# A macaron block on one core: folded sums, values loaded by fours, and finer first and last steps

## What is computed

```python
x = x + 0.5 * ffn(layernorm(x))
x = x + attention(layernorm(x))
x = x + 0.5 * ffn(layernorm(x))

def ffn(x):                    # up (2048, 512), down (512, 2048): only their signs are used
    hidden = relu((x @ sign(up).T) * up_scale)
    return (hidden @ sign(down).T) * down_scale * output_scale

def attention(x):              # 16 heads of 32
    q, k, v = heads(x @ w_q.T), heads(x @ w_k.T), heads(x @ w_v.T)
    return merge(softmax(q @ k.T / sqrt(32)) @ v) @ w_o.T

def layernorm(x):
    return (x - mean(x)) / sqrt(var(x) + 1e-5)
```

## Time and profile before

| | |
|---|---|
| median of 3 runs | 2874.53 us |
| the profiled execution | 2881.08 us |
| its span, first to last instruction | 2879.0 us |
| TensorE busy | 2846.1 us (99%) |
| weight loads | 1949.0 us (68%) |
| vector engine | 2041.4 us (71%) |
| scalar engine | 1607.7 us (56%) |
| POOL | 1372.8 us (48%) |
| DMA packets | 184375, 424.28 MB |

### The profile page before, as it was taken

The page is one execution under the profiler, slowest core; times in us unless marked ns, Lnnn a source line. Parts: engine busy times, 40 slices in busy tenths (PEclk is TensorE's granted clock), DMA queues, the critical chain, the costliest instruction groups (busy, mean ns, idle before and its releaser), DMA issues.

```text
span 2879.0 us, 37964 instructions
## 1 busy us (share of the span) xinstructions
PE 2846.1 (99%) x14288; PEld 1949.0 (68%) x14288; DVE 2041.4 (71%) x3037; ACT 1607.7 (56%) x2850; POOL 1372.8 (48%) x487
## 2 busy tenths in 40 slices
PE   8999999999999999999999999999999999999999
PEld 6888888887755555555555555555555468888887
DVE  5655556768888888888888888888888446555553
ACT  6344434332276767767677777676777654333333
POOL 0000000000089999989898899898988620000000
PEclk9999999999999999999999999999999999999999
DMA  5111112555389999999999999999999962222210
GB/s 190 31 58 30 30 30 71 200 194 188 136 175 194 200 203 202 201 200 203 201 202 204 197 203 202 201 200 200 203 200 204 209 179 59 59 59 59 59 30 30
DMA packets 184375, 424.28 MB, mean 147 GB/s; under 512 B 89728, under 2 KB 90752, under 8 KB 148224
## 3 DMA queue, kind: packets, MB, share of 16 engines
q0 software_dynamic: 31824, 231.75, 39.2%
q1 hardware_dynamic: 152368, 190.11, 24.1%
HBM read 121.91 MB, written 67.63 MB: 66 GB/s over the span
## 4 chain that ended last, share of the span: by engine, by line
PE 84%; DMA 7%; POOL 3%; DVE 3%; issue 2%; ACT 1%; SPq 0%; POOLq 0%; DVEq 0%; ACTq 0%
PE bank L624 16%; PE bank L601 15%; PE bank L1064 15%; PE bank L1060 13%; PE bank L1091 13%; PE bank L743 7%; DMA att_dma_acc<-att_p 3%; PE bank L451 3%; POOL att_acc L924 3%; DMA att_dma_acc<-att_dma_acc 2%; PE bank L1118 1%; DMA prob_sums<-head_total 1%; DMA head_tot_t<-prob_sums 0%; PE bank L240 0%; DMA op_inv_second<-prob_inverse 0%
## 5 line engine op out<-in xcount | busy, mean ns | idle before, releaser
L975 DVE TENSOR_REDUCE att_row_max<-bank 128x1 f32<-128x512 f32 x2048 | 1249.3, 681 | 209.3 <-PE bank L1064 209.1
L924 POOL TENSOR_TENSOR att_acc<-att_acc,att_p 128x2048 f32<-128x2048 f32 x217 | 1079.8, 4976 | 19.7 <-ACT att_p L1044 13.0
L1044 ACT ACTIVATE att_p<-bank 128x512 f32<-128x512 f32 x1792 | 919.4, 617 | 289.3 <-PE bank L1060 286.2
L1064 PE MATMUL bank<-att_k,att_q 96*128 96x512 f32 x2048 | 834.0, 409 | 2.9 <-DVE att_row_max L975 2.6
L1060 PE MATMUL bank<-att_q,att_k 98*128 98x512 f32 x2048 | 810.3, 399 | 6.0 <-ACT att_p L1044 6.0
L1064 PEld LDWEIGHTS bank<-att_k,att_q 96*128 96x128 f32 x2048 | 387.2, 189 | 275.0 <-DVE att_row_max L975 123.2
L1060 PEld LDWEIGHTS bank<-att_q,att_k 98*128 98x128 f32 x2048 | 386.8, 189 | 116.7 <-ACT att_p L1044 17.6
L573 ACT ACTIVATE ffn_hid<-bank,up_s 128x512 f32<-128x512 f32 x256 | 176.3, 689 | 517.2 <-PE bank L601 505.7
L521 DVE TENSOR_TENSOR ffn_hid_lo<-ffn_hid,ffn_hid_hi 128x512 fp32r<-128x512 f32 x256 | 175.7, 691 | 383.7 <-ACT ffn_hid_hi L576 383.7
L1091 PE MATMUL bank<-att_p,att_v 128*32 128x512 f32 x3584 | 434.6, 601 | 0.0
L601 PE MATMUL bank<-hi,ffn_up_w 128*128 128x512 f32 x1024 | 400.7, 391 | 5.7 <-DVE lo L189 3.8
(11 more groups left out here) (116 smaller groups left out, 2378.8 us busy)
## 6 DMA issues: line engine op xcount, KB each, us to landing
att_dma_acc<-att_p POOLq DMA_DIRECT2D x161, 1024.0 KB, 10.6
att_dma_acc<-att_dma_acc POOLq DMA_DIRECT2D x30, 1024.0 KB, 11.9
att_dma_acc<-att_acc POOLq DMA_DIRECT2D x30, 1024.0 KB, 6.9
att_q<-q_hi SPq DMA_DIRECT2D x64, 256.0 KB, 4.1
att_k<-k_hi SPq DMA_DIRECT2D x64, 256.0 KB, 6.7
x<-x_after_ffn SPq DMA_DIRECT2D x15, 1024.0 KB, 7.3
x_after_ffn<-x_out SPq DMA_DIRECT2D x8, 1024.0 KB, 9.9
q_hi<-qkv_o_hi SPq DMA_DIRECT2D x32, 256.0 KB, 2.0
```

What stands on the lines that cost most here:

```text
L924: self.nc.gpsimd.tensor_tensor(self.acc[H % 2][:], a[:], self.tile(H, kt)[:], ALU.add).then_inc(self.summed, 1)
L975: self.nc.vector.tensor_reduce(self.row_max[odd][:, qt, q:q + 1], m[:], axis=AX.X, op=ALU.max).then_inc(self.m_read, 1)
L1044: self.nc.scalar.activation(into[:, q * CH:(q + 1) * CH], self.score_bank(H, kt, q)[:], ACT.Exp, scale=SCALE).then_inc(self.exp_done, 1)
L1064: self.nc.tensor.matmul(m[:], self.q_st[T % NB][0:KQ, qt * P:(qt + 1) * P], self.k_st[T % NB][0:KQ, q * CH:(q + 1) * CH], start=True, stop ...
```

## The change

- Sums over partitions: for 1 < N < 8 and N > 17 (`folded`) the vector engine adds rows 64 to 127 of the sum to rows 0 to 63 (`fold`: add, copy of half the rows to the other half, add of half the rows), writes the high part to rows 0 to 63 and the low part to rows 64 to 127 of one tile (`parts`), and TensorE multiplies that once.
- First chunk: TensorE runs 13 and 9 products of the identity with itself before and after the first mean; the mean is one float32 product of the unsplit sum; the first signs are made in two halves, each ahead of a half of the high part; the norm's later steps stand one hidden tile later.
- First chunk of Q, K, V and of the second FFN: norm steps moved by one tile, later in the one, sooner in the other.
- Attention: values are loaded for four heads at once (`load_values`, eight loads of 1 MB, the first in the last chunk of Q, K, V), into other places; the six loads of Q and K for heads 0 and 1 are spread over tiles; the last head's tile 8 is summed by TensorE and no more by POOL; the output weights wait in another place.
- Second FFN: the load of down signs 4 stands ahead of head 30's sums on SP's queue; the input of the last chunk has a place of its own and is asked for earlier; in the last chunk the last two down groups are interleaved, and the last output tile is made and stored in two halves.

The core of the diff:

```diff
@@ class Norm
+    def folded(self, N, k):
+        return 1 < N < NCH or N > 2 * NCH + 1
+    def fold(self, dve, which):
+        which = sum(self.folded(i // 2, i % 2) for i in range(which))
+        nc, shifted = self.nc, self.work[0:ROWS, 0, :]
+        nc.vector.tensor_tensor(self.sum[:], self.work[:, 0, :], self.work[:, 1, :], ALU.add).then_inc(self.folding, 1)
+        dve.wait_ge(self.folding, 2 * which + 1)
+        nc.vector.tensor_copy(shifted, self.sum[ROWS:P, :]).then_inc(self.folding, 1)
+        dve.wait_ge(self.folding, 2 * which + 2)
+        return nc.vector.tensor_tensor(self.sum[0:ROWS, :], self.sum[0:ROWS, :], shifted, ALU.add)
+    def upper_part(self, N, k):
+        rows = slice(0, ROWS if self.folded(N, k) else P)
+        return self.nc.vector.tensor_copy(self.parts[rows, :], self.sum[rows, :])
+    def lower_part(self, N, k):
+        if self.folded(N, k):
+            return self.nc.vector.tensor_tensor(self.parts[ROWS:P, :], self.sum[0:ROWS, :], f32(self.parts[0:ROWS, :]), ALU.subtract)
+        return self.nc.vector.tensor_tensor(self.sum_lo[:], self.sum[:], f32(self.parts[:]), ALU.subtract)
@@ vector_first
-        nc.vector.tensor_tensor(self.sum[:], work[:, 0, :], work[:, 1, :], ALU.add).then_inc(self.dve, 2)
-        for k in (2, 3):
-            self.vector(dve, k, 0, None, None, None)
+        nc.vector.tensor_tensor(self.sum[:], work[:, 0, :], work[:, 1, :], ALU.add).then_inc(self.dve, 4)
@@ scalar_first
         for h in range(2):
+            make_half(act, h)
             act.wait_ge(self.first, 3 + h)
@@ Norm.tensor
-        nc.tensor.matmul(out[:], self.ones[:], self.sum_hi[:], start=True, stop=False)
-        nc.tensor.matmul(out[:], self.ones[:], self.sum_lo[:], start=False, stop=True).then_inc(self.pe, 1)
+        if N == 0 and k == 0:
+            nc.tensor.matmul(out[:], f32(self.ones[:]), self.sum[:], start=True, stop=True).then_inc(self.pe, 1)
+            return
+        ins = nc.tensor.matmul(out[:], self.ones[:], self.parts[:], start=True, stop=self.folded(N, k))
+        if not self.folded(N, k):
+            ins = nc.tensor.matmul(out[:], self.ones[:], self.sum_lo[:], start=False, stop=True)
+        ins.then_inc(self.pe, 1)
@@ Stream.input
-        return self.second if N == NCH + 1 else self.x[N % 2]
+        return self.second if N in (NCH + 1, 3 * NCH - 1) else self.x[N % 2]
@@ Ffn.steps, second FFN, n == 0
-            return ({8: (0, 1, 2, 3), 10: (4,), 11: (5, 6), 13: (7, 8, 9, 10), 15: (11,)},
+            return ({8: (0, 1, 2, 3), 10: (4,), 11: (5, 6), 12: (7, 8, 9, 10), 15: (11,)},
@@ Ffn.tensor
-            if (n, ht) == (0, 2) and not oproj:
+            if (n, ht) == (0, 3) and not oproj:
                 st.norm.tensor(pe, 1, N)
+                elif h == HT - 1:
+                    for dt in range(DT):
+                        self.down_products(h - 1, dt)
+                        self.down_products(h, dt).then_inc(self.last_ready, 1)
@@ Qkv.steps, n == 0
-            return ({2: (4,), 3: (5, 6), 4: (7, 8), 6: (9,), 8: (10, 11, 12, 13, 14, 15), 9: (16, 17)},
-                    {2: (0,), 6: (1,), 9: (2, 3)}, {2: 0, 6: 1})
+            return ({3: (4,), 4: (5, 6), 5: (7, 8), 7: (9,), 8: (10, 11, 12, 13, 14, 15), 9: (16, 17)},
+                    {3: (0,), 7: (1,), 9: (2, 3)}, {3: 0, 7: 1})
@@ pooled
-    return (0, 2, 8) if H == NH - 1 else ...
+    return (0, 2) if H == NH - 1 else ...
@@ class Attention
-        self.v_st = [c.sb(f"att_v{i}", at, [P, KT, HD]) for i, at in enumerate((HID_AT + 2, HID_AT, INV_AT))]
+        self.v_st = [c.sb(f"att_v{i}", at, [P, KT, P]) for i, at in enumerate((HI0_AT, LO0_AT, INV_AT))]
+    def load_values(self, sp, g):
+        first = HEADS_AT_ONCE * g
+        row, col = first % HEADS * HD, first // HEADS * SEQ
+        sp.dma_start(self.v_st[2 if g == VALUE_LOADS - 1 else g % 2][:],
+                     self.v_scr[col:col + SEQ, row:row + P].rearrange("(t p) d -> p t d", p=P)).then_inc(self.values_loaded[g % 2], 16)
@@ sync
-                            att.load(sp, 0)
-                        if n == 4 and t == 6:
-                            att.load(sp, 1)
+                        if n == 4 and 2 <= t < 5:
+                            att.load(sp, 0, (2 * t - 4, 2 * t - 3))
+                        if n == 5 and 2 <= t < 8:
+                            att.load(sp, 1, (t - 2,))
+                        if (n, t) == (NCH - 1, 2):
+                            att.load_values(sp, 0)
+                    if H % HEADS_AT_ONCE == 1 and H // HEADS_AT_ONCE + 1 < VALUE_LOADS:
+                        att.load_values(sp, H // HEADS_AT_ONCE + 1)
+                    if H == LAST:
+                        signs2.load(sp, 4)
                     if H > 0:
                         head_out.move_sums(sp, H - 1)
-                signs2.load(sp, 4)
+                    if n == NCH - 3:
+                        sp.wait_ge(oproj.scaled, NCH)
+                        st.load(sp, 3 * NCH - 1, x1)
@@ vector
-                    late = {0: norm.vector_first_squares, 3: norm_steps(0, 11), 4: norm_steps(0, 12), 5: norm_steps(0, 13, 14, 15)}
+                    late = {0: norm.vector_first_squares, 4: norm_steps(0, 11), 5: norm_steps(0, 12), 6: norm_steps(0, 13, 14, 15)}
@@ tensor
+                def keep_going(count):
+                    for _ in range(count):
+                        nc.tensor.matmul(c.bank[7][:, 0:P], ident[:], ident[:], start=True, stop=True)
+                keep_going(FIRST_TURNS)
                 norm.tensor(pe, 0, 0)
+                keep_going(SECOND_TURNS)
```

118 lines of the change are left out of this document (71 added, 47 removed).

## The result

The changed kernel takes 2858.64 us, the median of five runs (2857.39 to 2860.53), against 2875.59 us for the kernel before, run beside it: a ratio of 0.9943, with a 95% interval of 0.9931 to 0.9955. In a second set, beside other runs of before, its median was 2859.91 us and the ratio again 0.9943. The prediction was 2859.5 us, in a range of 2852 to 2868. The profiled execution took 2858.64 us, 2856.6 of them its span.

What follows compares the result with a forecast made beforehand. TensorE, busy 99% of the span, was taken as the bound, with excess matmuls, waits and low clock to win back. Terms of 5.8 + 2.2 - 0.4 + 3.5 + 2.2 + 0.7 + 0.7 + 0.3 = 15.0 us gave 2859.5 us, range 2852 to 2868.

Steps and rivals of the forecast that it cites:

- Folded sums: Both FFNs' sums over partitions: 24 matmuls fewer at 0.24 us, 5.8 us saved, the vector engine's extra work thinly covered.
- The rival with a dear copy: Folds in both FFNs: a dear copy between partitions makes the kernel slower, 2881 to 2892 us; chance 0.05.
- First chunk: Start of the first FFN: turns, unsplit mean and split signs bring step 4 forward; 2.2 us saved.
- First chunk of Q, K, V: Next norm's steps one tile later: waiting moves to the second sum and first product; 0.4 us lost.
- Loads of values: Q, K, V, chunk 4: moving the value load ends the stall for row maxima and its clock loss; 3.5 us saved.
- End of attention: Last head into second FFN: tile 8 off POOL (a) and earlier down signs (b), capped; 2.2 us saved.
- The uncapped sum: End of attention: (a), tile 8 on TensorE, and (b), earlier down signs, together would give 4.9 us.
- The cap: End of attention: POOL's up signs, tied to a DMA that doesn't move, limit the gain to 2.3 us.
- The large wait: Head 30: 5.4 us of waiting plus 5 us of clock stay, as nothing in the change touches them.
- the large wait goes too: Head 30: lighter traffic lands POOL's DMA earlier, 10 us more saved, 2849 us (2846 to 2853); chance 0.10.
- stalls are passed on: Start, chunk 4 and second FFN's start: stalls reappear elsewhere, 7.7 us saved, 2867 us (2864 to 2871); chance 0.28.
- Rest: Second FFN: 0.7 us for the last input, 0.7 for chunk 0's earlier sums, 0.3 for the last outputs.

Runs made afterwards that it cites:

- values_only: The kernel before with only the four-head value loads and the spread Q and K loads of heads 0 and 1: 2874.77 us, ratio 0.9988.
- no_turns: The kernel after without the unused identity products around the first mean, finer steps of the first chunk kept: 2859.93 us, ratio 0.9944.
- before_again: The kernel before, unchanged, profiled once more: one profiled execution of 2878.13 us, no interval.
- tile8_on_pool: The kernel after with tile 8 of the last head summed by POOL again, not by TensorE: 2864.61 us, ratio 0.9949.
- signs_in_old_place: The kernel after with the second FFN's last half of first-chunk down signs requested after the attention loop again: 2863.96 us, ratio 0.9957.

## Why the prediction came out right, and where it didn't

The sum of the terms was 15.0 us. The medians of before and after differ by 16.95 us in the one set and 15.97 in the other. Behind this stand two steps that failed in the same direction, each by some 2 us, and smaller ones that failed in the other. By steps:

*Folded sums, taken at 5.8.* The term was too small and its cover too hopeful: 24 x 0.29 = 7.0 us, less 1.3 us of waits on average, 5.7. The price of the copy, bounded in the prediction between half of 0.42 and 2.29, was 0.42. "The cover is thin" was the right warning, and one to four waits above 0.2 us did appear in six of eight profiles, by the length of the chunks. The rival with a dear copy is out.

*First chunk, taken at 2.2.* The two profiles of before and values_only have 77.4 to 78.0 us, the seven with nine turns 74.7 to 76.6, on average 75.8: 1.8 us. The first product came at 13.20 us, where 13.1 was said, but step 4 at 25.62, not 24.7, since the clock fell at 15 us, behind a pause of 2.35 us that nine turns didn't fill and one of 0.65. The gain isn't the warm clock that the term was built on: the finer steps alone bring 1.7 us, as no_turns shows. "0.5 per turn, no delay" doesn't add up (13 turns from 1.8 would end at 8.3, behind the sum at 7.7), but a turn took 0.36 us there, and TensorE stood 1.33 us. "Full clock at the first product" held, "at full clock the first group ends at 16.1" did not.

*First chunk of Q, K, V, taken at -0.4:* -0.5.

*Loads of values, taken at 3.5.* Mis-sized by the clock. The wait for the maxima went, and 0.4 to 0.8 us for K remained. But the 1.7 us of clock that the sum counted as part of the stall were lost in one profile of before and not in the other: 3.2 or 1.7 us. The 3.4 us by the ratio (0.3 to 6.6) and the 2.0 by the medians allow both.

*End of attention, taken at 2.2.* This step failed. The uncapped sum, 4.9 us, was right as far as one pair of profiles can say. The cap rested on "tied to a DMA that doesn't move". It did move: POOL's signs began at 2314.67 us before, 73.4 us behind the last transpose, after 3.65 us of waiting for their DMA, and in after so:

```profile
2301.49 5.71 POOL L379 TENSOR_SCALAR ffn_up_w<-x_out 128x2048 fp32r<-128x2048 f32 x1
```

That is 67.3 us behind the last transpose, right behind POOL's last move, with no wait. The DMA was issued 47.8 us behind the last transpose before and 44.0 after, and took 25.4 and 19.1 us to land; before_again and values_only have 24.9 and 25.5, the kernels with the rest of the change 19.1 to 23.2. In tile8_on_pool the signs began 67.2 us behind the transpose with POOL's add in place, and in signs_in_old_place 67.1, so neither of the two edits alone is what moved them; why this DMA lands sooner stays open. The two halves also don't add up as two terms: tile 8 is worth 3.2 us with the signs early, the signs are worth 1.7 with tile 8 on POOL (tile8_on_pool and before_again: 148.65 against 153.05 us from the last transpose to chunk 1, of the 4.4 us 2.0 are the wait in head 30 and 0.7 the earlier sums; TensorE's wait for the signs, 1.8 us in the first profile of before, is 0.9 in this one), and 8.3 in the profile (4 to 5 by the times) once tile 8 is off it.

*The large wait "stays" as something "nothing here touches".* It doesn't hang on any edit that was tried, but it didn't stay: POOL's lead is 0.6 to 1.9 us in three profiles of before and values_only and 3.5 to 6.8 in eleven with the rest of the change. It has two faces, and on average they left, with the end of attention, 72.8 us in the six profiles whose code behind the last transpose is that of after, where before and values_only have 78.6: 5.7 us, and 2.1 in chunk 0 of FFN 2. Taken off these 7.8 us: 4.9 of the uncapped sum and 0.7 for the earlier sums of chunk 0. Some 2.2 us remain for head 30. That was the rival "the large wait goes too" in small; its 10 us weren't to be had, because the low half waits behind it. The rival "stalls are passed on" (2864 to 2871 us) is out by both medians, though one of its stalls is there: tile 8 of chunk 4 does wait for K (0.7 us in after).

*Rest.* The x of the last chunk: chunks 1 to 6 of FFN 2 gained 420.8 - 416.3 = 4.5 us, 3.5 of them by the fold (419.82 to 416.34), so 1.0 for x, where 0.7 stood. The end: from the last product to the end 4.3 us before, 3.55 after, 0.75 instead of 0.3. The vector engine's last outputs in after, which answer to the earlier trace rows, and the last product:

```profile
2853.06 0.39 PE L634 MATMUL bank<-ffn_hid_lo,ffn_down_w 128*128 128x512 f32 x1
...
2852.58 0.75 DVE L602 SCALAR_TENSOR_TENSOR x_out<-bank,down_s,x_in_own_place 128x512 f32<-128x512 f32 x1 [0.15 <-PE bank L634]
2853.49 0.88 DVE L602 SCALAR_TENSOR_TENSOR x_out<-bank,down_s,x_in_own_place 128x256 f32<-128x256 f32 x2 [0.16 <-PE bank L634]
```

All stages of the table, as means over the profiles that share a stage's code, give 1.8 + 2.2 (chunks 1 to 6: 3.5 less 1.3) + 2.0 + 0.7 (heads, cause not shown) + 5.7 + 2.1 + 4.5 + 0.8 = 19.8 us, three more than the times: the two profiled executions of before, 2881.08 and 2878.13 us, lie 5.2 and 2.3 above the 2875.9 of most runs. The prediction took the saving off the median, and there it holds; its 2866 us for a profiled execution doesn't: these took 2858.64 and 2857.68.

So the mechanism was right in most terms. A cap that didn't hold (2.7 us too few) and a wait that shrank (2.2 too few) make 4.9 us; clock counted too high in the first chunk and in the loads takes back 1.5 of them. That 2859.5 us lies within 1 us of both medians is luck: by the stages the sum was nearly 5 us too small, and the times show only 16 to 17 of these 19.8 us, since the two profiled executions of before were longer than most.

What the lead hangs on can be read from the traces: on how long the adding DMA at the end of head 29 takes, for which POOL waits. POOL behind it in before, and in after:

```profile
2234.32 0.88 POOL L954 DMA_DIRECT2D att_dma_acc<-att_acc  x1 [5.64 <-DMA att_dma_acc<-att_dma_acc]
...
2223.50 0.87 POOL L1020 DMA_DIRECT2D att_dma_acc<-att_acc  x1 [2.38 <-DMA att_dma_acc<-att_dma_acc]
```

In the three profiles with the small lead POOL issues this DMA 22.8 to 23.0 us ahead of the last transpose, and it lands 14.1 to 15.3 us later; in the eight in the middle it does so 23.6 to 25.1 us ahead, and it takes 12.6 to 13.5; in the three with a lead of 6.7 to 6.8 us 26.1 to 26.4 us ahead, and it takes 8.6 to 10.1. SP's two loads of 1 MB for the end of attention go out 25.7 and 22.6 to 22.9 us ahead of that transpose in the first eleven. So a microsecond by which POOL comes there earlier gives nearly two of lead, and the DMA is shortest where it is out ahead of both loads.

What stays open is why POOL comes there later in before. Its place against the transposes wanders by some 3 us or more over the heads in every kernel, so part of it is chance; but three profiles against eleven don't mix, and neither the values, the signs, tile 8, the fold, the turns nor the steps in Q, K, V, taken back one at a time, bring the small lead back. Nothing in the loop of the first 30 heads differs between values_only and after.

## What to carry to other kernels

A wait is a race between two chains; before calling one untouched or capping a gain with it, ask which instruction sets the other chain's start, and whether the change moves that too. Two edits at the same wait are one term, not two: with one chain early, the other's old place cost 4 to 8 us instead of 2. And before a few microseconds are argued over, profile the same kernel twice: here one of the two largest waits, the clock behind another and the landing of an input differed by 1 to 2 us between executions of one program.
